# Feed-forward of a four-layer transformer sandwich: layer norm's scale and bias on VectorE, third gate matmul moved ahead of the sixth slot's norms

## The chip, the cores and the metric

The kernel runs on one core of one Trainium2 chip. The metric is the device time of one execution in microseconds (us). "PE" is TensorE, "ACT" ScalarE, "DVE" VectorE, "POOL" GpSimd, "SP" the engine whose queue issues the DMAs; "PEld" is TensorE's loading of weights, which runs beside its matmuls.

## The reference

Four sublayers work on x of shape 8 x 256 x 128, each as x = x + layernorm(f(layernorm(x))): additive attention, a stack of six local attention and feed-forward layers, a state space model, and a mixture of experts. The change lies in the stack, in its feed-forward part:

```python
for i in range(6):
    x = attn_layer(shift_tokens(x), Wqkv[i], q_scale[i], k_scale[i], Wo[i]) + x
    x = ffn_layer(shift_tokens(x), ln_g[i], ln_b[i], W1[i], b1[i], W2[i], b2[i]) + x

def ffn_layer(x, g, bln, W1, b1, W2, b2):
    mu = x.mean(-1, keepdims=True)
    var = ((x - mu) ** 2).mean(-1, keepdims=True)
    xn = (x - mu) / jnp.sqrt(var + 1e-05) * g + bln
    hg = xn @ W1 + b1
    a, gate = jnp.split(hg, 2, -1)
    return a * jax.nn.gelu(gate, approximate=False) @ W2 + b2
```

W1 gives 341 columns of a and 341 of the gate, which the kernel takes in three blocks of 128, 128 and 85 (f = 0, 1, 2).

## The kernel before, in words

Channels lie on the 128 partitions and tokens along the free dimension. The stack (`local_attention`) cuts the 2048 tokens into four units of 512. One iteration i is one unit of one layer, so there are 24 iterations, and each has eight slots j = 0 to 7, one for a pair of heads. `iterations` calls the same `slot` function for every engine; what an engine does is written out by hand in its own `slot`, and each engine executes its list strictly in order, waiting on semaphores (`need`, and on PE also `gather`).

The work is a software pipeline. In slot j PE makes the scores of pair j (L506, L514), projects q, k and v of pair j+2 (L480, L481, L471), mixes the values of pair j-2 (L539), makes the norms of pair j+2 (`norms`, L492) and turns the probabilities of pair j-1 (L524). ACT takes the exponentials of pair j (`exponential`, L688), copies and squares q and k of pair j+2 (`raw_copy`, L660 and L663), copies the mixed values and the new values (L695, L654), makes the inverse norms (`inverse_norm`, L670 and L672) and spreads the probabilities (L680 to L683). DVE makes the softmax's maximum and shift (`soft_a`, L814, L818), its sum and reciprocal (`soft_b`, L824, L827), multiplies q and k by the cosine table (`straight`, L798), multiplies by the inverse norms (`normalise`, L806) and scales the probabilities (`soft_c`, L833). POOL does two multiplies and adds of 128x1024 a slot for the rotary part (`turned`, L767 and L772); L767 waits for a DMA that shuffles the copy made by L660. The norms of PE wait for `sq` (L663) and for `straight` (L798), since they overwrite the PSUM banks that these read.

The feed-forward of unit k = i - 1 is spread over the same slots of iteration i. Slots 0 to 2: the output projection (L552) and the residual (L873). Slot 3: the mean (L559), on DVE the copy of the feed-forward's columns (L877, a small `tensor_scalar` into `f_fcol`) and the centring (L880). Slot 4: the square (L713), the variance (L563), its logarithm and exponential (L728, L730, the latter written into PSUM bank 3), and at the end of DVE's slot 4 the product xn = cen * rs (L884). Slot 5: ACT applies scale and bias in place to xn (L733), between `value_copy` and `inverse_norm`; PE makes the three gate matmuls (`gate_mm`, L570) at the very end of its slot, after `norms` and `turn`; ACT loads the table of Gelu and applies it three times (`gelu`, L701) as the last thing of its slot. Slot 6: `hid_mm` 0 and 1 (L579), on DVE `hidden` (L841). Slot 7: the rest of these, the second matrix (L586) and the residual (L888).

PSUM bank 2 is shared by the values (L471, read by L654) and gate block 0, bank 7 by the mix (L539, read by L695) and gate block 1, bank 3 by everything else of the feed-forward and gate block 2. So PE's values of slot 6 wait for a Gelu that has freed bank 2, its mix of slot 6 for one that has freed bank 7, and `hid_mm` for bank 3. These waits are counts of one semaphore, `gelu`, which each of the three Gelus raises by one.

Of the kernel before, what the change touches and what calls it, by code (L numbers as in the profile page):

```python
# [288 lines left out]
def need(eng, sem, value):  # L289

    if not isinstance(value, int) or value > 0:
        eng.wait_ge(sem, value)

def local_attention(nc, io, x, con):
# [9 lines left out]
    with Pool(nc) as m:  # L305
# [39 lines left out]
        tokens = lambda u, g: view(y, 2 * u * YB + g, [YB, 2], [1, S], p0=64 * g, rows=64)  # L345

        Y0, H0_, G0 = NU, 1, 1
        GBANK = (2, 7, 3)

        n2_out = o[:, T:2 * T]
# [103 lines left out]
        def _(pe):  # L455
# [6 lines left out]
            def values(i, m, q):  # L462

                need(pe, sem["y2"], i - NU + 1 + Y0)
                need(pe, sem[f"wv{q // 4}"], (i // NU) * 16 + 16)
                need(pe, sem["v"], i * 8 + q)
                if q == 0:
                    need(pe, sem["gelu"], i * 3 - 6 + 1 + G0)
                for b in range(2):
                    at = (2 * m + b) * YB + 64 * (q % 4)  # L470
                    mm = pe.matmul(view(ps, 2 * CH, [1, CH], p0=64 * b, rows=64), y[:, at:at + 64],  # L471
                                   wv[:, CH * (q // 4):CH * (q // 4) + CH], start=True, stop=True)
                mm.then_inc(sem["v_mm"], 1)
# [53 lines left out]
            def mix(i, j):  # L527

                gather(sem["ptz"], i * 8 + j + 1)
                gather(sem["o"], i * 8 + j)  # L530
                if j == 4:
                    gather(sem["gelu"], i * 3 - 3 + 2 + G0)
                if j % 4 == 0:
                    gather(sem["v"], i * 8 + j + 4)
                for p in range(4):
                    n = 96 if p < 3 else 64
                    for h in range(2):
                        for b in range(2):
                            mm = pe.matmul(view(ps, (6 + b) * CH + S * b + 64 * p, [1, n], p0=64 * h, rows=64),  # L539
                                           v[64 * b:64 * b + 64, p * INNER + 128 * j + 64 * h:p * INNER + 128 * j + 64 * h + 64],  # L540
                                           ptz[64 * b:64 * b + 64, 96 * (4 * h + p):96 * (4 * h + p) + n],
                                           start=(p == 0), stop=(p == 3), skip_group_check=True)
                mm.then_inc(sem["pv_mm"], 1)
# [19 lines left out]
                pe.matmul(bank(3), con.ones[:, :], sq2[:, :], start=True, stop=True).then_inc(sem["var"], 1)  # L563

            def gate_mm(i, f):
                if f == 0:
                    need(pe, sem["xn"], i + 1)
                    need(pe, sem["w1"], (i // NU) * 16 + 16)
                f0, n = FB[f]
                pe.matmul(view(ps, GBANK[f] * CH, [1, CH], rows=n), w1[:, DI + f0:DI + f0 + n], xn[:, :],  # L570
                          start=True, stop=True).then_inc(sem["g_mm"], 1)

            def hid_mm(i, f):
                if f == 0:
                    need(pe, sem["gelu"], i * 3 + 3 + G0)
                if f:
                    need(pe, sem["hid"], i * 3 + f + H0_)
                f0, n = FB[f]
                pe.matmul(view(ps, 3 * CH, [1, CH], rows=n), w1[:, f0:f0 + n], xn[:, :],  # L579
                          start=True, stop=True).then_inc(sem["h_mm"], 1)  # L580
# [9 lines left out]
            def slot(i, m, j, run, more, before):  # L590
                k = i - 1
                has, u, a = (run, i, j + 2) if j < 6 else (more, i + 1, j - 6)
                had1, u1, b1 = (run, i, j - 1) if j >= 1 else (before, k, 7)
                had2, u2, b2 = (run, i, j - 2) if j >= 2 else (before, k, j + 6)
                mu, mk = (m if j < 6 else (m + 1) % NU), (m - 1) % NU
                if run:
                    scores(i, j)
                if has:
                    project(u, mu, a)
                    values(u, mu, a)  # L600
                if had2:
                    mix(u2, b2)
                if before and j < 3:
                    wo_part(k, 3 * j, min(3 * j + 3, NP))
                if before and j == 3:
                    mean(k, mk)
                if before and j == 4:
                    variance(k)
                if before and j == 6:
                    hid_mm(k, 0)  # L610
                if before and j == 7:
                    hid_mm(k, 2)
                if has:
                    norms(u, a)
                if had1:
                    turn(u1, b1)
                if before and j == 5:
                    if run:
                        need(pe, sem["v"], i * 8 + 8)
                    gate_mm(k, 0)  # L620
                    gate_mm(k, 1)
                    gate_mm(k, 2)
                if before and j == 6:
                    hid_mm(k, 1)
                if before and j == 7:
                    w2_mm(k)
# [21 lines left out]
        def _(act):  # L648
# [48 lines left out]

            def gelu(i, f):
                n = FB[f][1]
                need(act, sem["g_mm"], i * 3 + f + 1)  # L700
                act.activation(gate[0:n, f * UNIT:f * UNIT + UNIT], view(ps, GBANK[f] * CH, [1, CH], rows=n),  # L701
                               ACT.Gelu, bias=fcol[0:n, 5 + f:6 + f]).then_inc(sem["gelu"], 1)

            def slot(i, m, j, run, more, before):
# [21 lines left out]
                if before and j == 4:  # L726
# [1 line left out]
                    act.activation(sq2[:, :], bank(3), ACT.Ln, bias=con.eps).then_inc(sem["ln2"], 1)  # L728
                    need(act, sem["ln2"], k + 1)
                    act.activation(bank(3), sq2[:, :], ACT.Exp, scale=-0.5).then_inc(sem["rs2"], 1)  # L730
                if before and j == 5:
                    need(act, sem["scaled"], k + 1)
                    act.activation(xn[:, :], xn[:, :], ACT.Identity, scale=fcol[:, 0:1], bias=fcol[:, 1:2]).then_inc(sem["xn"], 1)  # L733
                if has:
                    inverse_norm(u, a)
                if had1:
                    spread(u1, b1)
                if before and j == 5:
                    for f in range(3):
                        gelu(k, f)  # L740

            nc.scalar.preload_act_table_set(ACT_SET)
# [39 lines left out]
        def _(dve):  # L782
# [53 lines left out]
            def hidden(i, f):  # L836

                n = FB[f][1]
                need(dve, sem["h_mm"], i * 3 + f + 1)
                need(dve, sem["gelu"], i * 3 + f + 1 + G0)  # L840
                dve.scalar_tensor_tensor(out=hid[0:n, f * UNIT:f * UNIT + UNIT], in0=view(ps, 3 * CH, [1, CH], rows=n),  # L841
                                         scalar=fcol[0:n, 2 + f:3 + f], in1=gate[0:n, f * UNIT:f * UNIT + UNIT],
                                         op0=ALU.add, op1=ALU.mult).then_inc(sem["hid"], 1)

            def slot(i, m, j, run, more, before):
# [35 lines left out]
                if before and j == 4:  # L881
                    need(dve, sem["rs2"], k + 1)
                    need(dve, sem["fcol"], k + 1)
                    dve.tensor_tensor(xn[:, :], cen[:, :], bank(3), ALU.mult).then_inc(sem["scaled"], 1)  # L884
                if before and j == 7:
                    need(dve, sem["w2_mm"], k + 1)
                    for g in range(2):
# [831 lines left out]
```

## Time and profile before

| | |
|---|---|
| median of 3 runs | 2366.53 us (2365.16 to 2367.01) |
| profiled execution, its own time | 2368.98 us |
| its span | 2367.2 us, 65878 instructions |
| granted TensorE clock, mean | 0.972 |
| PE busy | 2123.9 us (90%) |
| ACT busy | 1753.6 us (74%) |
| DVE busy | 1585.3 us (67%) |
| POOL busy | 1096.7 us (46%) |

The profile is of one execution. The times in its rows are microseconds from the start of the span. The stack takes the span from about 85 to 1855 us; an iteration takes 71.4 to 74.1 us. Busy shares are means over stages: which engine the others wait for has to be read from the timelines of one iteration. The timelines in the section on the rows are of the iteration whose L884 starts at 1139.46 us, unless said otherwise.

### The profile page before, as it was taken

The numbers are of one execution on the slowest core, as the hardware profiler recorded it, in microseconds if no ns is written. First come the engines' busy times: TensorE is split into PE (matmuls) and PEld (weight loads), VectorE is DVE, ScalarE is ACT, GpSimd is POOL, SyncE is SP. The second block draws the span as 40 slices with busy tenths as digits, with TensorE's granted clock in tenths as the row PEclk, the third lists the DMA queues.
The fourth block names the chain that finished last, engine by engine and source line by source line (L and its number), as shares of the span: only waits on it lengthen the run. The fifth ranks groups of instructions, "written<-read, shape, count | busy, mean of one in ns | idle before, by whom it ended". The sixth has DMA issues, their size and how long they took to land. (4 is left out here: it accounts for less than half of the span.)

```text
span 2367.2 us, 65878 instructions
## 1 busy us (share of the span) xinstructions
PE 2123.9 (90%) x26476; PEld 1010.9 (43%) x26476; DVE 1585.3 (67%) x2054; ACT 1753.6 (74%) x2574; POOL 1096.7 (46%) x461
## 2 busy tenths in 40 slices
PE   8699999999999999999999999999998687678697
PEld 3244444444444444444444444444443222223365
DVE  5566676666676676666666766767665589998432
ACT  4688878888888888888888788888886565455443
POOL 0255555455555555555555555555552025565030
PEclk8899999999999999999999999999999889999799
DMA  0332233322323223332233222333221100000011
GB/s 23 109 108 86 93 107 99 102 90 95 115 89 105 90 95 113 101 95 91 87 118 104 92 91 86 115 103 100 87 90 47 41 0 0 0 0 1 19 35 37
DMA packets 102070, 181.03 MB, mean 76 GB/s; under 512 B 15904, under 2 KB 67504, under 8 KB 101680
## 3 DMA queue, kind: packets, MB, share of 16 engines
q1 hardware_dynamic: 101776, 176.83, 23.2%
q8 instruction: 219, 3.59, 0.6%
q14 instruction: 75, 0.61, 0.1%
HBM read 24.73 MB, written 1.05 MB: 11 GB/s over the span
## 5 line engine op out<-in xcount | busy, mean ns | idle before, releaser
L767 POOL TENSOR_TENSOR f_shuf<-f_shuf,f_tabs 128x1024 f32<-128x1024 f32 x192 | 467.7, 2436 | 866.0 <-DMA f_shuf<-f_raw 866.0
L772 POOL TENSOR_TENSOR f_rot<-f_rot,f_shuf 128x1024 f32<-128x1024 f32 x192 | 452.8, 2358 | 15.1
L814 DVE TENSOR_REDUCE f_max<-f_ps 128x8 f32<-128x512 f32 x192 | 132.7, 691 | 302.4 <-PE f_ps L514 294.5
L670 ACT ACTIVATE f_rn<-f_ps 128x1024 f32<-128x1024 f32 x192 | 195.9, 1021 | 134.0 <-PE f_ps L492 134.0
L798 DVE TENSOR_TENSOR f_rot<-f_ps,f_tabc 128x1024 f32<-128x1024 f32 x192 | 235.1, 1225 | 51.9 <-ACT f_raw L660 49.3
L492 PE MATMUL f_ps<-f_sq,f_same 64*64 64x256 f32 x3072 | 210.1, 388 | 44.1 <-DVE f_rot L798 43.5
L806 DVE SCALAR_TENSOR_TENSOR f_qk<-f_rn,f_rot 128x1024 f32<-128x1024 f32 x192 | 233.4, 1216 | 9.5 <-POOL f_rot L772 8.0
L672 ACT ACTIVATE f_rn<-f_rn,k_lift 128x1024 f32<-128x1024 f32 x192 | 220.6, 1149 | 6.3
L480 PE MATMUL f_ps<-y_t,f_wq 128*128 128x512 f32 x384 | 217.1, 647 | 8.3 <-issue 5.5
L1200 POOL TENSOR_TENSOR s_prod<-s_state,s_cs 128x1024 f32<-128x1024 f32 x64 | 151.7, 2370 | 146.9 <-DVE s_state L1278 146.9
L824 DVE TENSOR_REDUCE f_sum<-f_ps 128x8 f32<-128x512 f32 x192 | 132.7, 691 | 119.8 <-ACT f_ps L688 119.5
L663 ACT ACTIVATE f_sq<-f_raw 128x1024 f32<-128x1024 f32 x192 | 203.0, 1057 | 6.5
L471 PE MATMUL f_ps<-f_wv,y_t 128*64 128x512 f32 x768 | 207.5, 619 | 0.0
L660 ACT ACTIVATE f_raw<-f_ps 128x1024 f32<-128x1024 f32 x192 | 196.4, 1023 | 8.6 <-PE f_ps L481 8.6
L539 PEld LDWEIGHTS f_ps<-f_ptz,f_v 64*64 64x64 f32 x6144 | 134.9, 132 | 157.3 <-issue 157.3
L481 PE MATMUL f_ps<-y_t,f_wk 128*128 128x512 f32 x384 | 197.2, 595 | 0.0
L492 PEld LDWEIGHTS f_ps<-f_sq,f_same 64*64 64x64 f32 x3072 | 104.9, 132 | 193.6 <-issue 173.7
L688 ACT ACTIVATE f_ps<-f_s 128x512 f32<-128x512 f32 x192 | 116.2, 605 | 96.0 <-DVE f_s L818 95.4
L552 PE MATMUL f_ps<-f_o,f_wo 128*128 128x512 f32 x384 | 183.7, 611 | 0.9 <-DVE y_t L888 0.9
L514 PE MATMUL f_ps<-f_qk 64*32 64x64 f32 x12288 | 165.3, 224 | 0.0
L539 PE MATMUL f_ps<-f_ptz,f_v 64*64 64x96 f32 (+1 forms) x6144 | 161.2, 243 | 3.5 <-ACT f_gate L701 2.0
L1149 ACT ACTIVATE s_ps<-s_delta,s_aneg 128x1020 f32<-128x1020 f32 x64 | 71.4, 1115 | 115.5 <-DVE s_state L1278 110.1
(262 smaller groups left out, 3551.9 us busy)
## 6 DMA issues: line engine op xcount, KB each, us to landing
f_shuf<-f_raw SPq DMA_DIRECT2D x384, 256.0 KB, 2.4
f_rn<-f_rn SPq DMA_DIRECT2D x384, 128.0 KB, 2.4
e_w<-in_e_w SPq DMA_DIRECT2D x16, 256.0 KB, 2.9
f_wq<-in_f_wq SPq DMA_DIRECT2D x12, 256.0 KB, 3.4
f_wk<-in_f_wk SPq DMA_DIRECT2D x12, 256.0 KB, 4.1
f_wv<-in_f_wv SPq DMA_DIRECT2D x12, 256.0 KB, 4.0
f_wo<-in_f_wo SPq DMA_DIRECT2D x6, 512.0 KB, 4.8
f_w<-in_f_w SPq DMA_DIRECT2D x6, 341.0 KB, 4.1
```

What stands on the lines that cost most here:

```text
L471: mm = pe.matmul(view(ps, 2 * CH, [1, CH], p0=64 * b, rows=64), y[:, at:at + 64], wv[:, CH * (q // 4):CH * (q // 4) + CH], start=True, sto ...
L480: pe.matmul(pair_of(ps, 0), wq[:, 128 * j:128 * j + 128], shifted(m), start=True, stop=True)
L481: pe.matmul(pair_of(ps, CH), wk[:, 128 * j:128 * j + 128], shifted(m), start=True, stop=True).then_inc(sem["a_mm"], 1)
L492: mm = pe.matmul(view(ps, CH * b + S * t, [1, S], p0=to, rows=64), same_head[64 * h:64 * h + 64, 64 * h:64 * h + 64], sq[64 * h:64 * h + 6 ...
L539: mm = pe.matmul(view(ps, (6 + b) * CH + S * b + 64 * p, [1, n], p0=64 * h, rows=64), v[64 * b:64 * b + 64, p * INNER + 128 * j + 64 * h:p ...
L660: act.activation(view(raw, 0, [UNIT, 2], [1, UNIT]), bank(0, 2), ACT.Copy).then_inc(sem["raw"], 1)
L663: act.activation(sq[:, :], raw[:, :], ACT.Square).then_inc(sem["sq"], 1)
L672: act.activation(view(t, 0, [UNIT, 4], [1, S]), view(t, 0, [UNIT, 4], [1, S]), ACT.Exp, scale=-0.5, bias=con.lift).then_inc(sem["rn"], 1)
L767: pool.tensor_tensor(view(w, 0, [S, 4], [1, S]), view(w, 0, [S, 4], [1, S]), view(tab_s, 0, [S, 2], [0, 2], [1, S]), ALU.mult).then_inc(se ...
L772: pool.tensor_tensor(t[:, :], t[:, :], w[:, :], ALU.add).then_inc(sem["rot"], 1)
L798: dve.tensor_tensor(view(rot[j % 2], 0, [S, 4], [1, S]), view(ps, 0, [S, 4], [1, S]), view(tab_c, 0, [S, 2], [0, 2], [1, S]), ALU.mult).th ...
L806: dve.scalar_tensor_tensor(out=view(qk[j % 2], 0, [KOFF, 2], [1, UNIT]), in0=view(rn[j % 2], 0, [UNIT, 2], [1, UNIT]), scalar=1e12, in1=vi ...
```

## The change

On DVE, at the end of slot 4, the product xn = cen * rs becomes a `scalar_tensor_tensor` that also multiplies by the scale column, and after a wait for it a new `tensor_scalar` adds the bias column in place in xn and raises `xn`. On ACT the pass L733 and its wait go. On PE the gate matmul of block 2 (`GFIRST`) goes to slot 5 ahead of `norms`, after the mix, with the waits for `xn` and `w1`; blocks 0 and 1 stay at the end of the slot. ACT takes the Gelus in the order 2, 0, 1, and every wait on `g_mm` or `gelu` is counted anew: `values` of slot 6 waits for the second Gelu of the iteration instead of the first, the mix for the third instead of the second, `hid_mm` 0 for the first instead of the third.

```diff
--- before.py
+++ after.py
@@ -345,7 +345,7 @@
         tokens = lambda u, g: view(y, 2 * u * YB + g, [YB, 2], [1, S], p0=64 * g, rows=64)
 
         Y0, H0_, G0 = NU, 1, 1
-        GBANK = (2, 7, 3)
+        GBANK, GFIRST = (2, 7, 3), 2
 
 
         n2_out = o[:, T:2 * T]
@@ -465,7 +465,7 @@
                 need(pe, sem[f"wv{q // 4}"], (i // NU) * 16 + 16)
                 need(pe, sem["v"], i * 8 + q)
                 if q == 0:
-                    need(pe, sem["gelu"], i * 3 - 6 + 1 + G0)
+                    need(pe, sem["gelu"], i * 3 - 6 + 2 + G0)
                 for b in range(2):
                     at = (2 * m + b) * YB + 64 * (q % 4)
                     mm = pe.matmul(view(ps, 2 * CH, [1, CH], p0=64 * b, rows=64), y[:, at:at + 64],
@@ -529,7 +529,7 @@
                 gather(sem["ptz"], i * 8 + j + 1)
                 gather(sem["o"], i * 8 + j)
                 if j == 4:
-                    gather(sem["gelu"], i * 3 - 3 + 2 + G0)
+                    gather(sem["gelu"], i * 3 - 3 + 3 + G0)
                 if j % 4 == 0:
                     gather(sem["v"], i * 8 + j + 4)
                 for p in range(4):
@@ -563,7 +563,7 @@
                 pe.matmul(bank(3), con.ones[:, :], sq2[:, :], start=True, stop=True).then_inc(sem["var"], 1)
 
             def gate_mm(i, f):
-                if f == 0:
+                if f == GFIRST:
                     need(pe, sem["xn"], i + 1)
                     need(pe, sem["w1"], (i // NU) * 16 + 16)
                 f0, n = FB[f]
@@ -572,7 +572,7 @@
 
             def hid_mm(i, f):
                 if f == 0:
-                    need(pe, sem["gelu"], i * 3 + 3 + G0)
+                    need(pe, sem["gelu"], i * 3 + 1 + G0)
                 if f:
                     need(pe, sem["hid"], i * 3 + f + H0_)
                 f0, n = FB[f]
@@ -606,6 +606,8 @@
                     mean(k, mk)
                 if before and j == 4:
                     variance(k)
+                if before and j == 5:
+                    gate_mm(k, GFIRST)
                 if before and j == 6:
                     hid_mm(k, 0)
                 if before and j == 7:
@@ -619,7 +621,6 @@
                         need(pe, sem["v"], i * 8 + 8)
                     gate_mm(k, 0)
                     gate_mm(k, 1)
-                    gate_mm(k, 2)
                 if before and j == 6:
                     hid_mm(k, 1)
                 if before and j == 7:
@@ -697,7 +698,7 @@
 
             def gelu(i, f):
                 n = FB[f][1]
-                need(act, sem["g_mm"], i * 3 + f + 1)
+                need(act, sem["g_mm"], i * 3 + (f + 1) % 3 + 1)
                 act.activation(gate[0:n, f * UNIT:f * UNIT + UNIT], view(ps, GBANK[f] * CH, [1, CH], rows=n),
                                ACT.Gelu, bias=fcol[0:n, 5 + f:6 + f]).then_inc(sem["gelu"], 1)
 
@@ -728,15 +729,12 @@
                     act.activation(sq2[:, :], bank(3), ACT.Ln, bias=con.eps).then_inc(sem["ln2"], 1)
                     need(act, sem["ln2"], k + 1)
                     act.activation(bank(3), sq2[:, :], ACT.Exp, scale=-0.5).then_inc(sem["rs2"], 1)
-                if before and j == 5:
-                    need(act, sem["scaled"], k + 1)
-                    act.activation(xn[:, :], xn[:, :], ACT.Identity, scale=fcol[:, 0:1], bias=fcol[:, 1:2]).then_inc(sem["xn"], 1)
                 if has:
                     inverse_norm(u, a)
                 if had1:
                     spread(u1, b1)
                 if before and j == 5:
-                    for f in range(3):
+                    for f in (GFIRST, 0, 1):
                         gelu(k, f)
 
             nc.scalar.preload_act_table_set(ACT_SET)
@@ -837,7 +835,7 @@
 
                 n = FB[f][1]
                 need(dve, sem["h_mm"], i * 3 + f + 1)
-                need(dve, sem["gelu"], i * 3 + f + 1 + G0)
+                need(dve, sem["gelu"], i * 3 + (f + 1) % 3 + 1 + G0)
                 dve.scalar_tensor_tensor(out=hid[0:n, f * UNIT:f * UNIT + UNIT], in0=view(ps, 3 * CH, [1, CH], rows=n),
                                          scalar=fcol[0:n, 2 + f:3 + f], in1=gate[0:n, f * UNIT:f * UNIT + UNIT],
                                          op0=ALU.add, op1=ALU.mult).then_inc(sem["hid"], 1)
@@ -881,7 +879,10 @@
                 if before and j == 4:
                     need(dve, sem["rs2"], k + 1)
                     need(dve, sem["fcol"], k + 1)
-                    dve.tensor_tensor(xn[:, :], cen[:, :], bank(3), ALU.mult).then_inc(sem["scaled"], 1)
+                    dve.scalar_tensor_tensor(out=xn[:, :], in0=cen[:, :], scalar=fcol[:, 0:1], in1=bank(3),
+                                             op0=ALU.mult, op1=ALU.mult).then_inc(sem["scaled"], 1)
+                    need(dve, sem["scaled"], k + 1)
+                    dve.tensor_scalar(xn[:, :], xn[:, :], fcol[:, 1:2], None, ALU.add).then_inc(sem["xn"], 1)
                 if before and j == 7:
                     need(dve, sem["w2_mm"], k + 1)
                     for g in range(2):
```

## Rows read from the trace of the kernel before

**Rows 1.** The page, busy time, share of the span and instructions of TensorE.

```profile
PE 2123.9 (90%) x26476; PEld 1010.9 (43%) x26476; DVE 1585.3 (67%) x2054; ACT 1753.6 (74%) x2574; POOL 1096.7 (46%) x461
```

**Rows 2.** The waits: who waited for whom, us in total, times, longest.

```profile
PE f_ps L492 <- DVE f_rot L798: 43.5, 53, 1.5
...
PE f_ps L506 <- DVE f_s L833: 37.3, 35, 1.7
```

**Rows 3.** Timeline of PE: start us, us, line, tiles, [idle before <-releaser].

```profile
1145.36 1.09 PE L492 MATMUL f_ps<-f_sq,f_same 64*64 64x256 f32 x16 [1.11 <-DVE f_rot L798]
...
1146.88 2.75 PE L570 MATMUL f_ps<-f_xn,f_w 128*128 128x512 f32 x6
...
1152.57 1.08 PE L471 MATMUL f_ps<-f_wv,y_t 128*64 128x512 f32 x4
...
1159.21 0.38 PE L506 MATMUL f_ps<-f_maskb,f_identb 128*128 128x256 bf16 x2 [1.20 <-DVE f_s L833]
```

**Rows 4.** Timeline of ACT, the same iteration.

```profile
1142.40 0.61 ACT L688 ACTIVATE f_ps<-f_s 128x512 f32<-128x512 f32 x1
...
1145.90 0.81 ACT L733 ACTIVATE f_xn<-f_xn,f_fcol 128x512 f32<-128x512 f32 x1
1146.61 1.02 ACT L670 ACTIVATE f_rn<-f_ps 128x1024 f32<-128x1024 f32 x1
...
1151.09 1.83 ACT L701 ACTIVATE f_gate<-f_ps,f_fcol 128x512 f32<-128x512 f32 x3
...
1156.72 0.60 ACT L688 ACTIVATE f_ps<-f_s 128x512 f32<-128x512 f32 x1
```

**Rows 5.** Timeline of DVE, the same iteration.

```profile
1139.46 0.69 DVE L884 TENSOR_TENSOR f_xn<-f_cen,f_ps 128x512 f32<-128x512 f32 x1 [0.31 <-ACT f_ps L730]
1140.50 0.69 DVE L814 TENSOR_REDUCE f_max<-f_ps 128x8 f32<-128x512 f32 x1 [0.35 <-PE f_ps L514]
1141.22 0.69 DVE L818 TENSOR_TENSOR f_s<-f_ps,f_max 128x512 f32<-128x512 f32 x1
1143.05 0.69 DVE L824 TENSOR_REDUCE f_sum<-f_ps 128x8 f32<-128x512 f32 x1 [1.13 <-ACT f_ps L688]
...
1155.62 0.75 DVE L841 SCALAR_TENSOR_TENSOR f_hid<-f_ps,f_fcol,f_gate 128x512 f32<-128x512 f32 x1 [0.29 <-PE f_ps L579]
```

**Rows 6.** Timeline of POOL: first iteration, this one, the latest L767, the last.

```profile
201.72 2.36 POOL L767 TENSOR_TENSOR f_shuf<-f_shuf,f_tabs 128x1024 f32<-128x1024 f32 x1 [2.54 <-DMA f_shuf<-f_raw]
...
1139.15 2.36 POOL L767 TENSOR_TENSOR f_shuf<-f_shuf,f_tabs 128x1024 f32<-128x1024 f32 x1 [2.77 <-DMA f_shuf<-f_raw]
1141.59 2.36 POOL L772 TENSOR_TENSOR f_rot<-f_rot,f_shuf 128x1024 f32<-128x1024 f32 x1
...
1284.58 2.36 POOL L767 TENSOR_TENSOR f_shuf<-f_shuf,f_tabs 128x1024 f32<-128x1024 f32 x1 [3.66 <-DMA f_shuf<-f_raw]
...
1789.43 2.36 POOL L767 TENSOR_TENSOR f_shuf<-f_shuf,f_tabs 128x1024 f32<-128x1024 f32 x1 [2.71 <-DMA f_shuf<-f_raw]
```

**Rows 7.** One line, L877: duration ns min/median/max, first and last start us, forms.

```profile
L877 DVE TENSOR_SCALAR f_fcol<-f_cols x24: 161/164/2296, 193.7 to 1829.8; 128x9 f32 x20, 128x9 f32<-128x9 f32 x4
```

**Rows 8.** Timeline of all engines about one of the long L877.

```profile
336.76 2.88 POOL L767 TENSOR_TENSOR f_shuf<-f_shuf,f_tabs 128x1024 f32<-128x1024 f32 x1 [0.70 <-DMA f_shuf<-f_raw]
...
337.94 1.73 DVE L877 TENSOR_SCALAR f_fcol<-f_cols 128x9 f32 x1
...
339.58 0.67 DVE L880 TENSOR_TENSOR f_cen<-y_t,f_ps 128x512 f32<-128x512 f32 x1
339.72 2.37 POOL L772 TENSOR_TENSOR f_rot<-f_rot,f_shuf 128x1024 f32<-128x1024 f32 x1
```

**Rows 9.** One line, L1218 (state space stage): duration ns min/median/max.

```profile
L1218 DVE TENSOR_SCALAR s_delta<-s_left,s_cols x8: 540/542/1005, 1878.8 to 1898.9; 128x512 f32<-128x512 f32 x8
```

**Rows 10.** Timeline of all engines about the longest L1218.

```profile
1875.88 3.59 POOL L1194 CAST s_pick<-s_dx 96x4096 bf16<-96x4096 f32 x1 [73.88 <-DMA s_dx<-in_k_pick]
...
1878.75 1.00 DVE L1218 TENSOR_SCALAR s_delta<-s_left,s_cols 128x512 f32<-128x512 f32 x1 [2.85 <-ACT s_left L1117]
```

## The prediction

> **What bounds the kernel now.** I read the page first. PE is busy for 90% of the span, ACT for 74% [rows 1], so PE looks like the bound, and a matmul moved into idle time of PE looks like a gain. The waits say where PE still stands still: 43.5 us before the norms, for `straight` on DVE, and 37.3 us before the scores, for `soft_c` on DVE [rows 2]. The timeline of one iteration places both around this change. In slot 5 PE idles 1.11 us before L492, and before the scores of slot 7 it idles 1.20 us [rows 3]. I went through all 24 iterations: the first idle is 1.11 us in every one, the second 1.15 to 1.31 in all but the last, and from the start of L884 to the scores of slot 7 the times repeat to 0.1 us. So this stretch, which holds everything that the change touches, is set by something that is not PE, and what happens in it adds whole to the iteration.
>
> What sets it is a chain through ACT and DVE. The exponential of slot 5 starts at 1142.40 [rows 4]. Its end, 1143.01, releases the sum at 1143.05, 0.04 us later [rows 5]. Sum, reciprocal and `straight` follow, which release the norms at 1145.36 [rows 3]. The norms take 1.09, so their results are there at 1146.45, and ACT's L670 starts at 1146.61, pushed back a little by L733 (1145.90 to 1146.71; neighbours on one engine overlap by about 0.1) [rows 4]. From there ACT has no pause: L670, L672, the spread, the Gelu table, three Gelus from 1151.09, `raw_copy`, the exponential of slot 6 at 1156.72 [rows 4]. That releases slot 6's softmax on DVE, and that the scores of slot 7 at 1159.21 [rows 3]. After it the rest of the iteration follows from PE and from the copies that it feeds, so a shift there is carried on.
>
> **The change part by part.** Times are of the same iteration, in the order of the chain.
>
> *ACT loses L733.* 24 passes of 0.81 us; in the queue each costs 0.71 (1145.90 to 1146.61) [rows 4]. Off the path: L670 also needs the norms, which are done at 1146.45; with the 0.04 us of a release it can start at 1146.49. So 0.12 us of the 0.71 are gained and ACT idles for the rest. Its cover is the wait for the norms, and what is late next is the norms themselves.
>
> *PE: the gate matmul ahead of the norms.* Three take 2.75 us [rows 3], one 0.9. PE has 1.11 us of idle there [rows 3], and xn is ready long before in either case below. So the norms are not moved, and slot 5's tail is 0.9 shorter. That moves the scores of slot 6, but not the chain, since what follows waits for ACT: cost nothing, gain nothing. If that idle were gone it would put 0.9 us before the norms and take the same 0.9 away after them.
>
> *The Gelus in another order.* The values of slot 6 (L471, 1152.57 [rows 3]) wait for the second Gelu of the three instead of the first. Three take 1.83 us [rows 4], so about 0.6 each: the second ends 1.2 us after 1151.09, at 1152.3, before the values were made anyway. With all of ACT later by the shift found below (0.63), it ends at 1152.9, and the values wait until 1153.0, 0.4 later than before; `hidden` (L841, 1155.62 [rows 5]) comes 0.4 later, less than the 0.63 by which the exponential beside it is late. No cost on the path. The mix waits for the third, which ends 0.6 later, when the values still run.
>
> *DVE's product.* L884 takes 0.69; as a product with a scalar column I price it like L841, 0.75 [rows 5]. It ends at 1140.21, and the wait for its own result lets the bias pass start at 1140.25.
>
> *DVE's bias pass.* This is the term that decides. Free, a `tensor_scalar` of 128x512 takes 0.54 us with two scalar columns [rows 9]; one should take no more. Put behind L884 it would end at 1140.8 and move the maximum (L814) from 1140.50 to about 1140.7. The shift L818 would end at 1142.1 instead of 1141.91 [rows 5], still before the 1142.40 at which ACT is ready for it [rows 4]. Hidden, then, by 0.49 us of slack.
>
> But POOL is at work there. L767 starts at 1139.15 and runs to 1141.51, with L772 behind it at 1141.59 [rows 6]. The trace has the same kind of operation beside POOL. L877 is a `tensor_scalar` of nine columns; its median is 164 ns and its longest 2296 [rows 7]. The long ones, seven of 24, are just those that start while L767 runs. The one at 337.94 takes 1.73 us and ends at 339.67, 0.03 after L767's end at 339.64 (336.76 + 2.88); L880 overlaps its end by 0.09, and POOL's next operation starts behind it at 339.72 [rows 8]. The other 17 start with POOL idle. L1218 shows it at the width of the new pass: 0.542 free, 1.00 where POOL's cast runs until 1879.47, with its end at 1879.75, 0.28 after POOL's [rows 9, 10]. So a `tensor_scalar` from SBUF to SBUF waits for the end of the POOL operation that was there first. L884 itself, with one operand in PSUM, keeps its 0.69 beside L767 [rows 5, 6].
>
> The Trainium skill has a rule for this (SBUF — State Buffer, "Who interferes with whom"): the second pair of VectorE's SBUF ports is shared with GpSimd and locked for a whole instruction, and fp32 `tensor_scalar` in its two-port mode is among those that need it. The rows agree in all eight held cases. The same page, in "A bandwidth-pool intuition that's wrong", gives about 115 ns from the holder's end for a blocked GpSimd. If DVE paid that before its full 0.54, it would end 0.66 after POOL instead of 0.28, and the sum would be some 9 us larger. The measured 0.28 decides.
>
> So the bias pass ends at 1141.51 + 0.28 = 1141.79. The maximum starts 0.09 before that, at 1141.70 instead of 1140.50: 1.20 later. Of this the slack takes 1141.91 + 0.04 to 1142.40, that is 0.45. **The exponential is 0.75 us late**, and with it the sum, `straight` and the norms. L670 starts at 1146.49 + 0.75 = 1147.24, 0.63 later than before. Gelus, `raw_copy`, slot 6's exponential and slot 7's scores follow with 0.63.
>
> *Over the iterations.* The later L767 ends, the larger the loss. It starts at 201.72 in the first iteration (L884 0.3 us after it), at 1789.43 in the last of 23, latest at 1284.58 [rows 6], where it is 0.57 behind L884 and still ahead of the bias pass (0.79 behind). Counted from L884's start, it ends after 2.05 to 2.10 us in sixteen iterations, after 2.23 to 2.36 in five and after 2.94 and 2.99 in two; mean 2.19, against 2.05 here. In the 24th POOL has nothing to do. Sum: 23 x (0.63 + 0.14) = 17.7, say **18 us**. Bounds of the held pass: 0.03 behind POOL (L877 [rows 8]) gives 12 us, a full 0.54 behind it gives 24. I take 0.28, since L1218 has the new pass's size [rows 10].
>
> The profiled execution took 2368.98 us of its own, 2.4 over the median of 2366.53. Its sum is 2387; against the median I forecast 2384.5.
>
> **The rivals.**
>
> *Held, as above*: 0.80. For it, eight cases of eight; against it, only that L877 and L1218 are neither in place nor in this slot.
>
> *The pass is not held, or the freed ACT covers it*: 0.10. Not held: the exponential stays, L670 comes 0.12 earlier, 23 x 0.12 = 3 us faster, 2363.7. Covered: if L670 were bound by ACT's own queue and not by the norms, the 0.71 freed would stand against the 0.75 lost, 23 x (0.04 + 0.14) = 4 us, 2370.6. The point that decides: the exponential is late only if L767 ends after 1140.76 (1141.51 less the 0.75); it ends at 1141.51. For the cover speaks that L670 starts only 0.12 after the norms; against it, that the exponential makes these very norms late.
>
> *The ScalarE pass was on the path after all*: 0.05. The idle of PE in slot 5 is filled, ACT's queue shortens by its whole 0.71, 24 x 0.71 = 17 us, 2349.5. Against it: norms end at 1146.45, L733 at 1146.71.
>
> *POOL's next operation goes first*: 0.05. DVE then also waits for L772, 2.36 + 0.08 more, 23 x 2.44 = 56 us on top, 2440. Against it, L772 let L877 pass in rows 8.
>
> **How the numbers follow.** The forecast's own range, from the bounds above, is 2378 to 2391. I widen it to 2374 and 2394, for part of the delay taken up in slots that I took as carried on, and for shifts of POOL against DVE. Left out are the rivals with their 0.20. A difference of 0.2%, 4.7 us, is about what a measurement of this kernel can tell. Faster by more: 0.06 (ACT's pass, a bit of the unheld case). Within: 0.10. Slower: 0.84.
>
> **What would show it.** Right: a mean of about 1.7 us for the bias pass (1141.79 - 1140.25, and 0.14) where it would be 0.5 free, each ending 0.28 after an L767; ACT waiting before slot 5's exponential for the shift of DVE; PE's wait before slot 5's norms grown, less the gate matmul; an idle of some 0.6 us on ACT before L670 in place of L733; scores of slot 7 0.6 later from L884's start. Wrong: a bias pass of 0.5 us beside a running L767, an exponential at 2.94 after L884's start, or a delay that is there in slot 7 and gone before the next L884.

## The result and the profile after

The changed kernel takes 2381.52 us (median of 5 runs, 2378.96 to 2388.07) against 2367.01 (2365.16 to 2371.65, 5 runs) before: ratio 1.0062, 95% interval 1.0047 to 1.0077, so 11 to 18 us slower. Its profiled execution took 2379.35 us with a span of 2377.6, 10.4 more than the span before.

The product is now L882, the bias pass L885, the maximum L812, the shift L816, `straight` L796, the exponential L689, `inverse_norm` L671, Gelu L702, POOL's pair L765 and L770. First the bias pass, in the view of one line (duration in ns min/median/max):

```profile
L885 DVE TENSOR_SCALAR f_xn<-f_xn,f_fcol x24: 486/1561/1827, 199.1 to 1850.1; 128x512 f32<-128x512 f32 x24
```

It takes 0.49 us once, in the last iteration, where POOL has nothing to do, and 1.54 or more in the other 23. The timelines of DVE, POOL and ACT in one iteration, beside [rows 4 to 6]:

```profile
1145.04 0.75 DVE L882 SCALAR_TENSOR_TENSOR f_xn<-f_cen,f_fcol,f_ps 128x512 f32<-128x512 f32 x1 [0.32 <-ACT f_ps L731]
1145.83 1.55 DVE L885 TENSOR_SCALAR f_xn<-f_xn,f_fcol 128x512 f32<-128x512 f32 x1
1147.30 0.68 DVE L812 TENSOR_REDUCE f_max<-f_ps 128x8 f32<-128x512 f32 x1
```

```profile
1144.73 2.37 POOL L765 TENSOR_TENSOR f_shuf<-f_shuf,f_tabs 128x1024 f32<-128x1024 f32 x1 [2.95 <-DMA f_shuf<-f_raw]
1147.17 2.42 POOL L770 TENSOR_TENSOR f_rot<-f_rot,f_shuf 128x1024 f32<-128x1024 f32 x1
```

```profile
1148.73 0.60 ACT L689 ACTIVATE f_ps<-f_s 128x512 f32<-128x512 f32 x1 [0.62 <-DVE f_s L816]
...
1152.83 1.03 ACT L671 ACTIVATE f_rn<-f_ps 128x1024 f32<-128x1024 f32 x1 [0.49 <-PE f_ps L492]
```

L765 ends at 1147.10 and the bias pass at 1147.38, 0.28 later. The maximum starts 2.26 us after the product's start, where it was 1.04 [rows 5]; the exponential 3.69 instead of 2.94, and ACT, which had no pause there [rows 4], now waits 0.62 us for DVE. L671 starts at 7.79 instead of 7.15, with 0.49 of idle in L733's place. PE's timeline, beside [rows 3]:

```profile
1149.76 1.09 PE L570 MATMUL f_ps<-f_xn,f_w 128*85 128x512 f32 x2
1151.68 1.09 PE L492 MATMUL f_ps<-f_sq,f_same 64*64 64x256 f32 x16 [0.83 <-DVE f_rot L796]
...
1158.63 1.08 PE L471 MATMUL f_ps<-f_wv,y_t 128*64 128x512 f32 x4 [0.63 <-ACT f_gate L702]
...
1165.39 0.38 PE L506 MATMUL f_ps<-f_maskb,f_identb 128*128 128x256 bf16 x2 [1.15 <-DVE f_s L831]
```

The gate matmul lies in PE's idle, and 0.83 us of it are left. Slot 7's scores start 20.35 us after the product instead of 19.75.

Where the time came from, from the starts of the product in both traces: over the first 22 iterations 1602.8 us against 1587.7, +15.1; in them slot 7's scores come 0.67 us later in the mean, 22 x 0.67 = 14.7. The 23rd iteration takes 48.13 against 45.99, +2.1. Together +17.3. The spans of the profiled pair differ by 10.4, 7 us less, since all that lies outside happened to be shorter (the first product starts at 198.31 instead of 202.02, and the part after the last one takes 3.2 less), in stages that the change doesn't touch; in the profiled executions of this study the first product starts anywhere between 197.6 and 203.1.

### The profile page after: what moved, and what is told of

Read it like the earlier page. It is cut to its first block and busy times, and to the rows that moved or that the text cites. A ratio compares the mean times of both kernels' runs of the same rounds, so it can differ in the third digit from the quotient of the medians.

```text
span 2377.6 us, 65894 instructions
## 1 busy us (share of the span) xinstructions
PE 2122.8 (89%) x26476; PEld 1006.9 (42%) x26476; DVE 1625.6 (68%) x2078; ACT 1742.1 (73%) x2550; POOL 1093.6 (46%) x461
## 5 line engine op out<-in xcount | busy, mean ns | idle before, releaser
L765 POOL TENSOR_TENSOR f_shuf<-f_shuf,f_tabs 128x1024 f32<-128x1024 f32 x192 | 462.3, 2408 | 882.9 <-DMA f_shuf<-f_raw 882.9
L770 POOL TENSOR_TENSOR f_rot<-f_rot,f_shuf 128x1024 f32<-128x1024 f32 x192 | 454.5, 2367 | 15.0
L812 DVE TENSOR_REDUCE f_max<-f_ps 128x8 f32<-128x512 f32 x192 | 132.4, 690 | 273.8 <-PE f_ps L514 266.0
L671 ACT ACTIVATE f_rn<-f_ps 128x1024 f32<-128x1024 f32 x192 | 196.2, 1022 | 145.6 <-PE f_ps L492 145.6
L796 DVE TENSOR_TENSOR f_rot<-f_ps,f_tabc 128x1024 f32<-128x1024 f32 x192 | 235.2, 1225 | 67.4 <-ACT f_raw L661 65.1
L664 ACT ACTIVATE f_sq<-f_raw 128x1024 f32<-128x1024 f32 x192 | 203.1, 1058 | 6.5
L689 ACT ACTIVATE f_ps<-f_s 128x512 f32<-128x512 f32 x192 | 116.0, 604 | 111.4 <-DVE f_s L816 111.0
L1279 DVE TENSOR_TENSOR_SCAN s_state<-s_ps,s_state 128x1024 f32<-128x1024 f32 x64 | 146.6, 2290 | 15.0 <-ACT s_ps L1150 14.8
```

The source lines that it names most:

```text
L664: act.activation(sq[:, :], raw[:, :], ACT.Square).then_inc(sem["sq"], 1)
L671: act.activation(view(t, 0, [UNIT, 4], [1, S]), view(ps, 0, [S, 4], [1, S]), ACT.Ln, scale=float(2.0 ** 20)).then_inc(sem["ln"], 1)
L765: pool.tensor_tensor(view(w, 0, [S, 4], [1, S]), view(w, 0, [S, 4], [1, S]), view(tab_s, 0, [S, 2], [0, 2], [1, S]), ALU.mult).then_inc(se ...
L770: pool.tensor_tensor(t[:, :], t[:, :], w[:, :], ALU.add).then_inc(sem["rot"], 1)
L796: dve.tensor_tensor(view(rot[j % 2], 0, [S, 4], [1, S]), view(ps, 0, [S, 4], [1, S]), view(tab_c, 0, [S, 2], [0, 2], [1, S]), ALU.mult).th ...
```

## The experiments

Names: "after" is the changed kernel. The numbers "after the product's start" count from L882 or L884 in each iteration, as in the last section. A "drop" is a stretch in which TensorE is granted its lower clock. Where a cut moves work, the counts of the waits that belong to it are moved with it and aren't all shown.

### The pass reads PSUM

```diff
-                    dve.scalar_tensor_tensor(out=xn[:, :], in0=cen[:, :], scalar=fcol[:, 0:1], in1=bank(3),
+                    dve.scalar_tensor_tensor(out=bank(3), in0=cen[:, :], scalar=fcol[:, 0:1], in1=bank(3),
...
-                    dve.tensor_scalar(xn[:, :], xn[:, :], fcol[:, 1:2], None, ALU.add).then_inc(sem["xn"], 1)
+                    dve.tensor_scalar(xn[:, :], bank(3), fcol[:, 1:2], None, ALU.add).then_inc(sem["xn"], 1)
```

> The change with the bias pass reading PSUM: the product is written into bank 3, in place of the inverse root, and the tensor_scalar reads bank 3 and writes xn. Theory (a tensor_scalar from SBUF to SBUF waits for the running POOL operation; one that reads PSUM doesn't): the pass takes about 0.69 us beside POOL, the maximum starts about 1.4 us after the product's start instead of 2.3, the exponential of slot 5 at 2.94 to 2.95 as in the kernel before, the scores of slot 7 at 19.6 to 19.75. Time 2363 us, 3 to 4 below the kernel before. Rival (an extra pass on VectorE costs what it costs, wherever it reads): exponential late, time about 2380.

Measured: 2365.61 us, ratio to the kernel before 0.9986 (0.9975 to 0.9997). The timeline of DVE and POOL:

```profile
1139.11 2.36 POOL L765 TENSOR_TENSOR f_shuf<-f_shuf,f_tabs 128x1024 f32<-128x1024 f32 x1 [3.07 <-DMA f_shuf<-f_raw]
...
1140.21 0.75 DVE L885 TENSOR_SCALAR f_xn<-f_ps,f_fcol 128x512 f32<-128x512 f32 x1
...
1140.87 0.68 DVE L812 TENSOR_REDUCE f_max<-f_ps 128x8 f32<-128x512 f32 x1
```

The pass takes 0.75 us in every one of 24 cases, in the middle of POOL's L765. The exponential is back at 2.95, slot 7's scores at 19.61, 0.13 before the mean of the kernel before. The same computation with the same number of passes, and the whole loss is gone: it isn't the extra pass that costs, but the pass that reads and writes SBUF while POOL works.

### The pass left out

```diff
-                                             op0=ALU.mult, op1=ALU.mult).then_inc(sem["scaled"], 1)
-                    need(dve, sem["scaled"], k + 1)
-                    dve.tensor_scalar(xn[:, :], xn[:, :], fcol[:, 1:2], None, ALU.add).then_inc(sem["xn"], 1)
+                                             op0=ALU.mult, op1=ALU.mult).then_inc(sem["xn"], 1)
```

> The change without its bias pass: the layer norm's bias isn't added in the feed-forward. Theory: with the held pass gone the exponential of slot 5 starts at 2.95 again and slot 7's scores at 19.6 to 19.7: 2363 us, the same as with the pass reading PSUM. Rival (the loss lies in the product with the scale, or in the matmul's place): stays at 2375 or more.

Measured: 2364.11 us, ratio 0.9982 (0.9970 to 0.9993), exponential at 2.95, slot 7's scores at 19.60. So the product with the scale costs nothing that can be measured, and neither does the pass that reads PSUM (2365.61): its 0.75 us lie in the slack ahead of the exponential.

### The kernel before without its ScalarE pass

```diff
-                    act.activation(xn[:, :], xn[:, :], ACT.Identity, scale=fcol[:, 0:1], bias=fcol[:, 1:2]).then_inc(sem["xn"], 1)
```

The wait of this pass goes too, and the product raises `xn` itself.

> The kernel before without its ScalarE pass: scale and bias of the layer norm are left out of the feed-forward. Theory: the norms bind L670, so only 0.08 to 0.12 us an iteration are gained, 2 to 3 us: about 2364. Rival (ScalarE's queue is the bound, the pass is worth its whole 0.71 us): 17 us, 2350.

Measured: 2366.14 us, ratio 0.9996 (0.9979 to 1.0012). The timeline of ACT:

```profile
1146.28 0.59 ACT L654 ACTIVATE f_v<-f_ps 128x512 f32<-128x512 f32 x1
1147.36 1.02 ACT L670 ACTIVATE f_rn<-f_ps 128x1024 f32<-128x1024 f32 x1 [0.49 <-PE f_ps L492]
```

L670 starts at 7.05 after the product, 0.10 earlier than before, and ACT now waits 0.49 us for the norms in the pass's place. A pass of 0.81 us, 24 times, was worth nothing that can be measured.

### A shorter POOL operation

```diff
+                if j == 6:
+                    pool.tensor_tensor(view(w, 0, [S, 2], [1, S]), view(w, 0, [S, 2], [1, S]),
+                                       view(tab_s, 0, [0, 2], [1, S]), ALU.mult).then_inc(sem["turned"], 1)
```

The `j` of `turned` is the pair; pair 6 is turned in slot 4. For the other pairs the operation stays as it is.

> The change with POOL's multiply of slot 4 on half its columns (the other half of this pair's rotary part isn't multiplied by the sine table). The operation that is running when the bias pass comes ends at about 0.9 us after the product's start instead of 2.05. Theory (held until the end of that operation): the bias pass ends at about 1.2, the exponential of slot 5 is back at 2.95, time 2363 to 2366. Rival (the pass is slow beside POOL in any case, or is held also by the next operation): exponential late, time 2380 or more.

Measured: 2363.34 us, ratio 0.9981 (0.9969 to 0.9994). The timeline of DVE and POOL in the first iteration:

```profile
198.40 1.28 POOL L766 TENSOR_TENSOR f_shuf<-f_shuf,f_tabs 128x512 f32<-128x512 f32 x1 [2.61 <-DMA f_shuf<-f_raw]
...
199.47 0.49 DVE L889 TENSOR_SCALAR f_xn<-f_xn,f_fcol 128x512 f32<-128x512 f32 x1
...
199.75 2.43 POOL L774 TENSOR_TENSOR f_rot<-f_rot,f_shuf 128x1024 f32<-128x1024 f32 x1
```

With the new passes untouched and only POOL's operation made shorter, the pass isn't late enough to matter: the maximum starts at 1.18 to 1.54 and the exponential at 2.95, and the loss is gone. The next POOL operation, 0.07 after the end of the first, doesn't hold it.

### Two passes, one behind the other

```diff
+                    need(dve, sem["scaled"], 2 * k + 2)
+                    dve.tensor_scalar(xn[:, :], xn[:, :], 1.0, None, ALU.mult).then_inc(sem["xn"], 1)
```

> The change with a second pass over xn behind the bias pass, a tensor_scalar that multiplies by one, also from SBUF to SBUF. The first pass ends 0.28 us after the POOL operation that held it. Theory A (whoever is waiting when the holder ends goes next; the second pass comes when POOL's next operation is already under way): the second pass is held for that whole operation, 2.4 us, slot 5's maximum starts near 4.9 after the product's start, and the time rises by 2.6 x 23 = 60 us, to about 2442. Theory B (DVE keeps its turn): the second pass takes 0.5 us, time near 2391.

Measured: one run, 2476.79 us. The timeline of DVE and POOL:

```profile
1200.49 2.36 POOL L765 TENSOR_TENSOR f_shuf<-f_shuf,f_tabs 128x1024 f32<-128x1024 f32 x1 [3.18 <-DMA f_shuf<-f_raw]
...
1201.50 1.64 DVE L885 TENSOR_SCALAR f_xn<-f_xn,f_fcol 128x512 f32<-128x512 f32 x1
1202.93 2.42 POOL L770 TENSOR_TENSOR f_rot<-f_rot,f_shuf 128x1024 f32<-128x1024 f32 x1
1203.17 2.46 DVE L887 TENSOR_SCALAR f_xn<-f_xn 128x512 f32<-128x512 f32 x1
1205.56 0.68 DVE L812 TENSOR_REDUCE f_max<-f_ps 128x8 f32<-128x512 f32 x1
```

Theory A holds: the second pass finds L770 under way and ends 0.28 after it (1205.63 against 1205.35); the maximum starts at 4.75 to 5.14 after the product in 22 iterations and at 5.56 in the 23rd. Two operations of 0.5 us each become 1.6 and 2.5. The size was missed: 95 us over after instead of 60. The scores of slot 7 come 3.8 us later in the mean than in after, where the hold accounts for 2.6. The rest comes together with drops of TensorE's clock: PE now idles 3.16 us before slot 5's norms, and the granted clock falls to 0.5 beside 19 of these 22 idles, where after has no drop in them. No run parts the two here; the next experiments do it for a shorter idle.

### The gate matmul back

```diff
-                if before and j == 5:
-                    gate_mm(k, GFIRST)
...
                     gate_mm(k, 0)
                     gate_mm(k, 1)
+                    gate_mm(k, 2)
...
-                    for f in (GFIRST, 0, 1):
+                    for f in range(3):
```

> The change with the third gate matmul back at the end of slot 5 and the Gelus in their old order; the passes stay on VectorE. Theory: the bias pass is held just the same, exponential of slot 5 at about 3.7 us after the product's start; the PE is 0.9 us later in slot 6, so that slot 6's sum on VectorE becomes bound by the hidden block instead of by ACT, which adds 0.1 to 0.2 us an iteration: time 3 us above the change, about 2385. Rival (the move of the matmul or the new order of the Gelus causes the loss): time near the kernel before, 2367.

Measured: 2403.63 us (2394.41 to 2408.80), ratio 1.0145 (1.0122 to 1.0168): 22 us over after, where I expected 3. The exponential is at 3.70, as in after, so the hold is the same. The timeline of PE in the first iteration:

```profile
205.51 1.50 PE L492 MATMUL f_ps<-f_sq,f_same 64*64 64x256 f32 x16 [1.86 <-DVE f_rot L795]
206.95 1.11 PE L524 MATMUL f_ps<-f_ident,f_s 128*128 128x128 f32 x4
207.85 3.55 PE L570 MATMUL f_ps<-f_xn,f_w 128*128 128x512 f32 x6
```

and in a later one:

```profile
1166.07 1.09 PE L492 MATMUL f_ps<-f_sq,f_same 64*64 64x256 f32 x16 [1.86 <-DVE f_rot L795]
1167.10 0.66 PE L524 MATMUL f_ps<-f_ident,f_s 128*128 128x128 f32 x4
1167.59 2.74 PE L570 MATMUL f_ps<-f_xn,f_w 128*128 128x512 f32 x6
```

The same matmuls take 1.50, 1.11 and 3.55 us in one and 1.09, 0.66 and 2.74 in the other. The view by stretches says why (length, busy time and count of PE, PEld, DVE, ACT and POOL, then the granted clock as a share of full speed, and the DMA's share and GB/s):

```profile
205.50:211.20 5.70, 5.69 (x26) 2.80 (x27) 1.60 (x2) 4.76 (x8) 2.85 (x2) 0.70 0.29 99
1159.50:1166.00 6.50, 4.66 (x106) 2.27 (x104) 5.71 (x8) 5.80 (x9) 4.42 (x2) 1.00 0.21 54
1166.00:1170.10 4.10, 4.03 (x26) 2.08 (x27) 1.66 (x2) 3.57 (x7) 2.37 (x1) 1.00 0.29 117
```

### A throwaway matmul in the idle

To tell the clock from the order of the work, the last version got one matmul more, which does nothing useful:

```diff
+                    need(pe, sem["xn"], k + 1)
+                    need(pe, sem["w1"], (k // NU) * 16 + 16)
+                    pe.matmul(view(ps, 3 * CH, [1, CH], rows=85), w1[:, DI + 256:DI + 341], xn[:, :], start=True, stop=True)
                 if has:
                     norms(u, a)
```

> The version with the gate matmul back and the held bias pass, plus one throwaway matmul of the third gate block ahead of slot 5's norms, whose result is made again later. It adds 24 matmuls of 0.9 us. Theory A (idle of PE lowers the clock): the 1.86 us of idle are cut to about 0.9, the granted clock stays at full speed in the iterations, and the time falls from 2403 to about 2385 although work was added. Theory B (order and place of the work): no fall, 2403 or more.

Measured: 2383.61 us (2380.78 to 2389.35), ratio 1.0068 (1.0049 to 1.0086). The same iteration as the slow one above:

```profile
203.26 1.09 PE L616 MATMUL f_ps<-f_xn,f_w 128*85 128x512 f32 x2
205.19 1.09 PE L492 MATMUL f_ps<-f_sq,f_same 64*64 64x256 f32 x16 [0.84 <-DVE f_rot L799]
206.21 0.66 PE L524 MATMUL f_ps<-f_ident,f_s 128*128 128x128 f32 x4
206.71 2.74 PE L570 MATMUL f_ps<-f_xn,f_w 128*128 128x512 f32 x6
```

The granted clock is at full speed in all 22 iterations, and 24 added matmuls make the kernel 20 us faster. Theory A holds: the idle lowered the clock. Of the 22 us that the moved gate matmul is worth in after, 20 come with the idle that it fills; 2 are left for PE's shorter list.

### PSUM pass, gate matmul back

The two edits above together (the pass reads PSUM; gate and Gelus in their old places).

> The bias pass reads PSUM, and the third gate matmul and the Gelus are back in their old places. Nothing is held, so PE's idle before slot 5's norms is 1.11 us, as in the kernel before. Theory A (with the gate back, TensorE's clock fell to 0.5 in about 12 of 22 iterations because PE stood idle for 1.86 us instead of 1.11): no drop of the clock in the stack's iterations here, slot 6's scores at 10.0 after the product's start, slot 7's at 19.7, time 2365, within 3 us of the version with the gate moved. Theory B (the gate's old place is bad by itself once the passes are on VectorE): some 20 us more, 2385.

Measured: 2364.89 us, ratio 0.9991 (0.9980 to 1.0002). PE idles 1.11 us before the norms and the granted clock has no drop in the 22 iterations. (With the gate back and the pass held, the profile has nine drops behind slot 5's idle and two in slot 4; my "about 12" was too many.) It can't be told from the version with the gate moved, 0.9986: without the hold, the move is worth nothing that these runs can tell.

### Looking for a faster version

The hold is also in the kernel before, in L877 [rows 7]. Here the columns' copy goes to ScalarE, on top of the pass that reads PSUM:

```diff
-                    dve.tensor_scalar(fcol[:, :], cols[:, bass.ds((k // NU) * 13 + 4, 9)], 1.0, None, ALU.mult).then_inc(sem["fcol"], 1)
...
+                if before and j == 3:
+                    need(act, sem["gelu"], k * 3 + G0)
+                    need(act, sem["y2"], k + Y0)
+                    act.activation(fcol[:, :], cols[:, bass.ds((k // NU) * 13 + 4, 9)], ACT.Copy).then_inc(sem["fcol"], 1)
                 if has:
                     inverse_norm(u, a)
```

On VectorE the line goes with its wait, and ScalarE's Gelus get a wait for `fcol`.

> The version whose bias pass reads PSUM, and the copy of the feed-forward's columns (L877 of the kernel before, a tensor_scalar from SBUF to SBUF on VectorE, held by POOL in seven to eight of 24 iterations for 1.6 us or more) is made by ScalarE in slot 3 instead, where ScalarE waits for the norms. Theory: ScalarE isn't held by POOL (the copy takes about 0.2 us), nothing is on the path, and the part of the held copies that reached the end goes: 1 to 5 us below the version that reads PSUM, about 2362. Rival (those holds were all absorbed by slack): no difference, 2365.

Measured: 2357.95 us, ratio 0.9958 (0.9942 to 0.9975). The line, and below it the same line on VectorE in the version that reads PSUM:

```profile
L736 ACT ACTIVATE f_fcol<-f_cols x24: 203/211/213, 191.6 to 1817.7; 128x9 f32 x20, 128x9 f32<-128x9 f32 x4
...
L875 DVE TENSOR_SCALAR f_fcol<-f_cols x24: 160/163/2281, 192.9 to 1830.4; 128x9 f32 x20, 128x9 f32<-128x9 f32 x4
```

It gave 7.7 us over the PSUM version by the medians, 6.6 by the ratios, more than the 1 to 5 expected; the 22 iterations take 1579.7 us instead of 1587.1. The PSUM version's profile has seven held copies of 1.73 to 2.28 us, some 12 us over their free 0.16 in all. The seven iterations that they lie in are the ones that became shorter, by 0.7 to 1.5 us each and 7.3 together; the other 15 differ by up to 0.5 either way and by 0.1 in sum. So more than half of the held time had reached the end.

The Gelu order in one iteration, alone and on top of this:

```diff
-                    for f in (GFIRST, 0, 1):
+                    for f in ((GFIRST, 1, 0) if run and not more else (GFIRST, 0, 1)):
```

The waits of the mix and of `hidden` for the Gelus are counted anew in that iteration.

> The version whose bias pass reads PSUM, with the Gelu order 2, 1, 0 in that one iteration alone. Theory: 1.5 us below 2365.6, about 2364, the iteration of 48.0 us back at about 46.5.

> As the version with the columns copied by ScalarE, and in the last iteration but one of the feed-forward (where no projection of a next unit covers the mix) the Gelus go 2, 1, 0, so that the mix waits for the second and not the third. Theory: that iteration returns from 48.0 us to about 46.5, so 1.5 us below the run beside it, about 2360.5.

Measured: alone 2365.40 us, ratio 0.9984 (0.9971 to 0.9996), not to be told from 0.9986, although the iteration is back at 46.34 us. On top of the columns' copy 2356.70, ratio 0.9951 (0.9932 to 0.9969), with that iteration at 47.45 instead of 48.47: the best version, 0.5% below the kernel before; that this last edit has a part in it isn't shown.

## Why the prediction was right

The chain from the held pass to slot 7's scores held link by link. Two steps beside it that the prediction had put at nothing did cost something, and the size came out partly by luck. By the prediction's own steps:

- **The bias pass is held by POOL.** Predicted: end 0.28 after L767's end, maximum 1.20 late. Measured 0.28, and 1.22 late (2.26 against 1.04). The PSUM pass, the short POOL operation and the pass left out each remove the loss; the rival that it is not held falls.
- **The exponential 0.75 late.** Measured 0.75 (3.69 against 2.94).
- **L670 0.63 late, of ScalarE's 0.71 only 0.12 gained.** Measured 0.64 late in after; without the pass and without the hold 0.10 gained. The rival that ScalarE's pass was on the path, with 2349.5 us, falls with 2366.14. The cover by the freed ACT (2370.6) falls as well: L671 isn't bound by ACT's queue, it waits 0.49 us for the norms.
- **POOL's next operation first.** It didn't go first in any of 23 iterations. The two passes show the one case found in which it does: when it is under way before VectorE's pass comes.
- **The rule of the Trainium skill** (SBUF — State Buffer, "Who interferes with whom"), by which a two-port `tensor_scalar` and a GpSimd operation lock each other out for a whole instruction: the trace agrees, with 0.28 behind POOL and 0.75 unheld from PSUM. The 115 ns from the holder's end, which the same page of the Trainium skill gives in "A bandwidth-pool intuition that's wrong" and which I had weighed against it, didn't come on top: the end stays at 0.28.
- **The size.** 17.7 us predicted for the loop, 17.3 measured there in the profiled pair (14.5 between the medians of all runs), but not by the same terms. The mean over the first 22 iterations was 0.67 and not 0.77, because L765 ended at 2.32 after the product at the latest (mean 2.10), where before it had ended twice at 2.94 and 2.99 (mean 2.19); such late ones differ from run to run (two at 2.76 with the throwaway matmul). That is 2 us less than predicted, and the 23rd iteration, with 2.1 instead of 0.77, made up for most of it: that the two cancel is luck.
- **Two readings of the rows.** From the start of L884 to slot 7's scores the kernel before takes 19.70 to 19.89 us, so it repeats to 0.2 us and not to 0.1. And its trace has a ninth held `tensor_scalar`, L1257 in the state space stage, so the count of eight left out one. It agrees that the pass is held, but it is 128x1024 wide and ends 0.55 behind POOL; that 0.28 was the right value rests on L1218's having the new pass's width.
- **What I missed, first: the Gelu order in the last iteration but one.** The step said that the mix waits for the third Gelu while the values still run, no cost. In the 23rd iteration there are no values of a next unit. PE waits 3.37 us before that mix instead of 2.02, and the matmuls behind it run at the lower clock. The kernel before, then after:

```profile
1802.93 0.84 PE L539 MATMUL f_ps<-f_ptz,f_v 64*64 64x96 f32 x32 [2.02 <-ACT f_gate L701]
1803.70 1.12 PE L579 MATMUL f_ps<-f_xn,f_w 128*128 128x512 f32 x2
...
1815.55 0.84 PE L539 MATMUL f_ps<-f_ptz,f_v 64*64 64x96 f32 x32 [3.37 <-ACT f_gate L702]
1816.32 2.06 PE L579 MATMUL f_ps<-f_xn,f_w 128*128 128x512 f32 x2
```

  The iteration costs 2.1 us more. With the new order it still takes 48.02 when the pass is left out; with the old order it takes 45.96 when nothing is held and 46.96 when the pass is held (throwaway matmul). So in after some 1.2 of the 2.1 go with the order and 1.0 with the hold.
- **Second: the gate matmul, "cost nothing, gain nothing".** Wrong in the presence of the hold. By filling the idle it keeps the clock up, worth 20 us; without the move the change would have cost 36 (2403.63 against 2367.82 beside it). The working took PE's durations as fixed, while the hold lengthened an idle on which they turned out to depend. The forecast was right because both edits came together; for the held pass alone it would have missed by 18 us.

## What to carry to other kernels

Before a pass goes from ScalarE to VectorE, look at what GpSimd runs at that moment. In these traces an fp32 `tensor_scalar` from SBUF to SBUF waits for the end of the whole GpSimd operation that was running before it (0.49 us free, 1.54 to 1.83 held), while one that reads PSUM does not (0.75 in all 24), though it is slower by itself. A pass that is taken off an engine is worth only what its successor doesn't wait for anyway; ask what releases the successor. And an idle of TensorE can have a second price, in its clock: here a matmul put into an idle of 1.86 us, even a useless one, paid 20 us.

## What the runs showed that I had not expected

- Nine drops of the granted clock behind an idle of about 1.86 us and two in slot 4, where the kernel before, after and the version with the throwaway matmul, with 1.11 and mostly about 0.84, have none: 20 us, more than the hold that made the idle (15 us). The one idle alone doesn't decide: the clock dropped behind nine of 22 much alike. In the first 22 iterations, over the traces of all versions, each of the 32 drops (11 with the gate matmul back, 19 with two passes, two with the shorter POOL operation, both in slot 4) lies beside an idle of 1.63 us or more, and such idles without a drop occur as well. What else goes in was not tried.
- A hold of 1.6 us or more on an operation over nine columns per partition, seven times in a run, was worth some 7 us. As a mean of its group (0.66 us, in a line with a median of 0.164) it was hard to see; the maximum in the view of the line shows it.
- A POOL operation behind a held pass starts in the records 0.07 after the one before, and is only 0.06 us longer (2.42 against 2.36): the hold costs DVE a microsecond and POOL next to nothing.
- How far behind the POOL operation a held pass ends goes with its width: 0.03 us for nine columns (L877), 0.28 for 512 (L885, L1218), and, from the two cases below, about 0.15 for 256 (the cosine table, in after) and 0.55 for 1024 (L1257, in the kernel before).

```profile
354.70 2.35 POOL L770 TENSOR_TENSOR f_rot<-f_rot,f_shuf 128x1024 f32<-128x1024 f32 x1
356.57 0.64 DVE L787 TENSOR_SCALAR f_tabc<-f_basec,f_cols 128x256 f32<-128x256 f32 x1
...
2047.20 3.23 POOL L1200 TENSOR_TENSOR s_prod<-s_state,s_cs 128x1024 f32<-128x1024 f32 x1 [1.22 <-DVE s_state L1278]
2048.27 2.71 DVE L1257 TENSOR_SCALAR s_delta<-s_delta 128x1024 f32<-128x1024 f32 x1
```
